# A spectral-routing block with experts on one core: the images of the first stage are normalised by ScalarE, large memsets move behind the folds, and the routing rows take a way through DRAM

## What is computed

```python
# block 1: x = x + conv_ref(layernorm over channels of x)
r = relu(conv1x1(x, rw_fc1)); r = relu(conv1x1(r, rw_conv)); r = conv1x1(r, rw_fc2)
routeing = softmax(r.mean(h, w).reshape(B, 4, 256), axis=1)
s = conv3x3(relu(conv3x3(x, sp_fc1)), sp_fc2)
spatial_routeing = softmax(s.mean(h, w).reshape(B, 4, 256), axis=1)
xp = star_scale * square(relu(x @ w_pw1.T)) + star_bias      # 128 -> 256 channels
xf = rfft2(xp)
weight = einsum('bfc,hwf->bhwc', routeing, complex_weights)
spatial_weight = einsum('bfc,hwf->bhwc', spatial_routeing, spatial_weights)
out = (xp * spatial_weight + irfft2(xf * weight)) @ w_pw2.T  # 256 -> 128 channels
# block 2: t = t + sum over the top 2 of 8 experts of softmax weight * w2(silu(w1 x) * (w3 x))
```

## Time and profile before

| | |
|---|---|
| median of 3 runs | 529.23 us (526.0 to 530.99) |
| span of the profiled execution, first to last instruction | 477.8 us |
| median less that span (what lies around it) | 51.4 us |
| first Fourier matmul of pair 0 | 25.05 us |
| the same of pair 5 | 74.95 us |
| `r_hl` complete | 115.6 us |
| first matmul of the second stage | 130.19 us |

### The profile page before, as it was taken

How to read it: one execution, slowest core, us unless ns; L and a number is a source line. 1 busy time by engine, 2 the same in 40 slices (tenths; PEclk the granted TensorE clock), 3 DMA queues, 4 the chain that set the end, 5 groups by cost and what they waited for, 6 DMA issues and landing times.

```text
span 477.8 us, 8130 instructions
## 1 busy us (share of the span) xinstructions
PE 359.2 (75%) x2236; PEld 292.9 (61%) x2237; DVE 272.9 (57%) x673; ACT 162.8 (34%) x374; POOL 260.3 (54%) x267
## 2 busy tenths in 40 slices
PE   0899999895199988875007699999999999998500
PEld 0555555393058777764006599887987888887400
DVE  5367675614077999996898554444434444433245
ACT  0454543302013223211400355443444444443253
POOL 7333342512176655541650667777777777777444
PEclk9999999978579999999555599999999999998955
DMA  8920000000200000004600111111111111112194
GB/s 249 248 63 1 2 0 0 1 5 9 35 1 1 23 22 32 34 24 152 287 0 1 45 40 54 50 52 49 54 51 49 55 50 49 52 54 50 42 358 162
DMA packets 14081, 29.94 MB, mean 63 GB/s; under 512 B 4392, under 2 KB 5564, under 8 KB 13548
## 3 DMA queue, kind: packets, MB, share of 16 engines
q1 hardware_dynamic: 7388, 17.93, 12.1%
q0 software_dynamic: 4784, 9.52, 6.7%
q10 hardware_dynamic: 1888, 2.23, 1.3%
HBM read 20.24 MB, written 8.85 MB: 61 GB/s over the span
## 4 chain that ended last, share of the span: by engine, by line
PE 35%; DVE 26%; DMA 13%; issue 12%; POOL 8%; ACT 2%; DVEq 1%; POOLq 1%; SPq 1%; ACTq 0%
PE bank L927 8%; DVE xn L964 7%; DMA y_dram<-shared,idx_s 7%; PE bank L909 6%; PE bank L902 3%; DMA RS<-r_hl 3%; PE bank L772 2%; PE bank L715 2%; PE bank L723 2%; POOL shared L490 2%; DVE st L954 2%; DMA shared<-tn_dram,idx_g 2%; PE bank L734 2%; DVE spec L1179 2%; PE bank L888 2%
## 5 line engine op out<-in xcount | busy, mean ns | idle before, releaser
L518 POOL DMA_INDIRECT shared<-tn_dram,idx_g x71 | 68.8, 968 | 39.9 <-DVE idx_g L1217 18.6
L527 POOL DMA_INDIRECT y_dram<-shared,idx_s x71 | 70.0, 986 | 27.1 <-issue 12.8
L909 PE MATMUL bank<-spec,shared 128*128 x426 | 61.2, 280 | 1.8 <-DVE shared L1233 0.7
L1247 DVE TENSOR_TENSOR shared<-shared,bank 128x384 f32<-128x384 f32 x71 | 39.3, 554 | 36.4 <-ACT shared L672 35.4
L672 ACT ACTIVATE shared<-bank 128x384 f32<-128x384 f32 x71 | 34.8, 490 | 64.3 <-PE bank L927 64.3
L909 PEld LDWEIGHTS bank<-spec,shared 128*128 128x128 f32 x426 | 53.5, 193 | 5.1 <-issue 5.0
L927 PE MATMUL bank<-RS,xgt_hl 128*128 x142 | 55.5, 391 | 0.6
L964 DVE TENSOR_SCALAR xn<-T,mv,rstd 128x128 f32<-128x128 f32 (+1 forms) x64 | 51.4, 874 | 5.1 <-POOL rstd L429 4.6
L927 PE MATMUL bank<-w_hi,xgt_hl 128*128 x142 | 48.9, 345 | 0.0
L427 POOL TENSOR_SCALAR var_eps<-mv 128x4 f32<-128x4 f32 x16 | 3.7, 229 | 68.7 <-DVE mv L958 68.6
L1228 DVE TENSOR_TENSOR xgt_hl<-bank,xgt_hl 128x128 fp32r<-128x128 f32 x71 | 20.6, 290 | 33.7 <-ACT xgt_hl L660 33.7
(11 more groups left out here) (171 smaller groups left out, 680.0 us busy)
## 6 DMA issues: line engine op xcount, KB each, us to landing
star<-y_dram SPq DMA_DIRECT2D x16, 256.0 KB, 5.4
star<-in_w SPq DMA_DIRECT2D x2, 1536.0 KB, 8.5
tn_dram<-xn SPq DMA_DIRECT2D x8, 256.0 KB, 2.0
out<-T ACTq DMA_DIRECT2D x8, 256.0 KB, 2.3
spec<-in_w SPq DMA_DIRECT2D x1, 1536.0 KB, 13.2
shared<-in_sp_even SPq DMA_DIRECT2D x1, 1280.0 KB, 13.2
shared<-tn_dram,idx_g POOLq DMA_INDIRECT x71, 2.5
y_dram<-shared,idx_s POOLq DMA_INDIRECT x71, 2.2
```

The lines of the kernel that those rows point to most:

```text
L518: pool.indirect_dma_start(xg[b], None, tn_dram, bass.IndirectOffsetOnAxis(ap=idx_g[quad][:, col:col + 1], axis=0)).then_inc(S[f"g_x{b}"], 16)
L527: pool.indirect_dma_start(y_dram, bass.IndirectOffsetOnAxis(ap=idx_s[quad][:, col:col + 1], axis=0), yo[b], None).then_inc(S[f"y_out{b}"], 16)
L909: mm = pe.matmul(p_y[:, 0:DIM], hidt[u][:, c * P:(c + 1) * P], w2s[:, c, ds(e * DIM, DIM)], start=(c == 0), stop=(c == HC - 1))
L1247: dve.tensor_tensor(hid[u], silu[u], p_h3[u][:, 0:HID], ALU.mult).then_inc(S["f_act"], 1)
```

## The change

Four things are done. (1) ACT writes `xn` in the first stage, as an activation with a scale `rstd` and a bias `shift` = -mean * rstd; POOL computes `neg_mean` and `shift`, two more small operations for each pair. DVE's `normalise` goes from the first stage and stays in the second. (2) ACT does one relu of one column into `table_probe` behind its first four DMAs, so that its table is loaded there. (3) POOL's large memsets, among them that of `RS` (now in two halves), move from ahead of the first fold to behind the folds of pairs 0 and 1. (4) The routing rows go from `r_hl` into a DRAM buffer `r_dram` by two DMAs of 128 KB, and from there into `RS` by four DMAs of 128 KB, each into 8 partitions; all six are issued by SP.

```diff
+        r_dram = nc.dram_tensor("r_dram", (2, 2, NF, PAIRS * 4 * P), F32).ap()
-        def routing_rows(eng, blocks, done):
-            eng.wait_ge(S["r_hi"], 1)
-            eng.wait_ge(S["r_lo"], 1)
-            eng.wait_ge(S["rs_zero"], 1)
-            for r in blocks:
-                eng.dma_start(RS[4 * r:4 * r + 4].rearrange("f c g b m -> f (c g b) m").bitcast(F32),
-                              r_hl[:, r % 2, 1 - r // 4, :].bitcast(F32)).then_inc(S[done], 16)
...
@@ SP @@
-            routing_rows(sp, range(5), "r_rows")
+            sp.wait_ge(S["r_hi"], 1)
+            sp.wait_ge(S["r_lo"], 1)
+            for s in (1, 0):
+                sp.dma_start(r_dram[s].rearrange("h f (x m) -> (f x) h m", m=P), r_hl[:, :, s, :].bitcast(F32))\
+                    .then_inc(S[f"r_out{s}"], 16)
+            sp.wait_ge(S["rs_zero"], 2)
+            for s in (1, 0):
+                sp.wait_ge(S[f"r_out{s}"], 16)
+                for half in range(2):
+                    r0 = 16 * (1 - s) + 8 * half
+                    sp.dma_start(RS[r0:r0 + 8].rearrange("r c g b m -> r (c g b m)").bitcast(F32),
+                                 r_dram[s].rearrange("h f n -> (h f) n")).then_inc(S["r_rows"], 16)
...
@@ POOL @@
                 wait_apart(pool, S[aggr], i + 1)
+                if aggr == "a_aggr":
+                    pool.tensor_scalar(neg_mean[:, u, :], mv[:, u, :, 0], -1.0, None, ALU.mult)
...
+            def neg_shift(i, u):
+                wait_apart(pool, S["a_rstd"], i + 1)
+                pool.tensor_tensor(shift[:, u, :], neg_mean[:, u, :], rstd[:, u, :], ALU.mult).then_inc(S["a_shift"], 1)
+
             def phase_a(i, u):
                 if not last(i, PAIRS):
                     inv_std("a_aggr", "a_eps", "a_rstd", LN_C_EPS, i + 1, 1 - u)
+                    neg_shift(i + 1, 1 - u)
...
-            routing_rows(pool, range(5, 8), "r_rows_pool")
             fold_rows(PAIRS - 1, 1)
...
@@ ACT @@
+            act.wait_ge(S["mhalf_set"], 1)
+            act.activation(table_probe[:, :], mhalf[:, 0:1], ACT.Relu)
             act.wait_ge(S["w_zero"], 3)
             for g in range(2):
                 act.dma_start(rwc[HALF * g:HALF * g + HALF, HALF * g:HALF * g + HALF], io["rwc"])\
                     .then_inc(S["consts_in"], 16)
+            def normalise_image(i, u):
+                act.wait_ge(S["a_shift"], i + 1)
+                for t in range(4):
+                    op = act.activation(xn[:, u, t, :], flat(T[:, ds(i * 4 + t, 1), :]), ACT.Identity,
+                                        scale=rstd[:, u, t:t + 1], bias=shift[:, u, t:t + 1])
+                op.then_inc(S["a_norm"], 1)
...
             def phase_a(i, u):
+                if not last(i, PAIRS):
+                    wait_done(act, S["a_tr"], i)
+                    normalise_image(i + 1, 1 - u)
                 if not deferred(i):
                     star_relu(i)
                     star_square(i)
...
@@ DVE, phase_a @@
-                if not last(i, PAIRS):
-                    wait_done(dve, S["a_tr"], i)
-                    normalise("a", i + 1, 1 - u)
```

More of the change, by code:

```diff
@@ L206, in metaformer @@
         var_eps = sb("var_eps", [P, 2, 4])
+        neg_mean = sb("neg_mean", [P, 2, 4])
+        shift = sb("shift", [P, 2, 4])
+        table_probe = sb("table_probe", [P, 1])
         tri = sb("tri", [P, P], F16)
@@ L326, in metaformer @@
             "ident_in consts_in tab_in x_in0 x_in1 x_in2 x_in3 route_in w1_in w3_in w2_in w_hi w_lo pad_zero coef_zero mhalf_set coef_ps "
-            "coef_hi coef_lo coef_in a_stats a_aggr a_eps a_rstd a_norm a_tr a_xc a_xp a_pw a_conv a_rw1 a_relu_s "
+            "coef_hi coef_lo coef_in a_stats a_aggr a_eps a_rstd a_shift a_norm a_tr a_xc a_xp a_pw a_conv a_rw1 a_relu_s "
             "a_relu_r a_rw2 a_rsum a_rows a_relu a_sq a_star a_fold a_dft a_spec r_cols r_full r_taps r_mm "
-            "r_log r_max r_sub r_exp r_sum r_rec r_norm r_tr r_hi r_lo r_rows r_rows_pool b_w b_sw b_p b_cross b_u b_y "
+            "r_log r_max r_sub r_exp r_sum r_rec r_norm r_tr r_hi r_lo r_out0 r_out1 r_rows b_w b_sw b_p b_cross b_u b_y "
             "b_vt b_vts b_w2 b_t b_stats b_aggr b_eps b_rstd b_norm b_tn0 b_tn1 b_tr b_tnt "
@@ L446, in _ @@
             inv_std("a_aggr", "a_eps", "a_rstd", LN_C_EPS, 0, 0)
+            neg_shift(0, 0)
+            phase_a(0, 0)
             pool.memset(coef[:].rearrange("p c k -> p (c k)").bitcast(F32), 0.0).then_inc(S["coef_zero"], 1)
@@ L454, in _ @@
                                pattern=[[-1, P]], channel_multiplier=1).then_inc(S["q_tri"], 1)
-            pool.memset(RS[:].rearrange("p c g b m -> p (c g b m)").bitcast(F32), 0.0).then_inc(S["rs_zero"], 1)
+            rs_flat = RS[:].rearrange("p c g b m -> p (c g b m)").bitcast(F32)
+            pool.memset(rs_flat[:, 0:2048], 0.0).then_inc(S["rs_zero"], 1)
+            phase_a(1, 1)
+            pool.memset(rs_flat[:, 2048:4096], 0.0).then_inc(S["rs_zero"], 1)
             pool.memset(tap_k[:].rearrange("p t b -> p (t b)"), 0.0).then_inc(S["k_zero"], 1)
             pool.memset(rw_k[:, :], 0.0).then_inc(S["k_zero"], 1)
-            pair_loop(pool, phase_a)
+            with pool.Fori(1, PAIRS // 2 - 1) as n:
+                for u in range(2):
+                    phase_a(n * 2 + u, u)
+            phase_a(PAIRS - 2, 0)
+            phase_a(PAIRS - 1, 1)
             pool.wait_ge(S["a_conv"], PAIRS)
@@ L598, in phase_a @@
                                accum_out=rsum[:, ds(i, 1)]).then_inc(S["a_rsum"], 1)
+            normalise_image(0, 0)
             act.wait_ge(S["pad_zero"], 1)
@@ L784, in _ @@
             pe.wait_ge(S["coef_in"], 16 * 8)
-            pe.wait_ge(S["r_rows"], 16 * 5)
-            pe.wait_ge(S["r_rows_pool"], 16 * 3)
+            pe.wait_ge(S["r_rows"], 16 * 4)
             pe.wait_ge(S["a_relu"], 2 * PAIRS)
@@ L1001, in _ @@
             stats("a", 0, 0)
-            normalise("a", 0, 0)
             pair_loop(dve, phase_a)
```

## The result

The changed kernel takes 545.78 us (median of 4 runs, 539.11 to 546.9) beside 529.45 for the kernel before in the same comparison: ratio 1.0294, 95% interval 1.0226 to 1.0363. It is slower, by 16.3 us; the forecast was 542. Its profiled execution spans 543.1 us.

What follows compares the result with a forecast made beforehand. It took a first-stage ring through statistics, POOL, DVE's `xn` and PE as the bound, with PE nearly so. Start -2.7, ring +15.3, last pass +1.1 and rows -1 gave +12.7: span 490.5 plus 51.4, 542 us; range 533 to 551.

Steps and rivals of the forecast that it cites:

- The ring: First stage: relus waiting for the next pair's `shift` join both paths into one ring, 13.05 us a pass, +15.3 us.
- the first rival: First stage: with relus free of `shift`, the old ring shrinks to 9.1 us a pass, 521 us in all; chance 5%.
- One sign: First-stage loop: PE idle some 4 us a pass, listed among the signs that the prediction is right.
- The clock: First stage: rival that PE's clock falls in some passes, a pass growing by 2 or so, +7 us, 549 us; chance 12%.
- the forecast case: Whole kernel: the prediction's main case, +12.7 us, 542 us; chance 55%.
- The start: Top of the kernel: first `star_matmul` at 12.1 instead of 14.81, held by the landing of the constants, -2.7 us.
- Memsets behind the folds cost nothing: First two folds: memsets of 3.1 and 2.7 us fit into POOL's 3.6 us idle from fold to next means.
- Behind the last pass: Pair 7, statistics to transposes after the last ring pass: 5.0 us instead of 3.93, +1.1.
- The routing rows: From `r_hl` to the filters' matmul: 13.2 us instead of 14.6 by way of DRAM, taken as -1 us.
- The rival of the quick rows: Routing rows: the 512 B pieces were the limit, so the routing saves 8 us instead of 1, 535 us; chance 18%.
- the price by partitions: Reads into `RS`: 8 partitions at a time give 54 GB/s, 2.4 us for 128 KB, 9.7 for four in turn.
- The 51.4 us around the span: Whole run: 51.4 us between the profiled span of 477.8 and the median of 529.23, taken as unchanged.

Runs made afterwards that it cites:

- e_norm_only: Kernel before with only the first stage's normalisation moved to ACT, ahead of the relus, with its two POOL operations: 494.31 us, ratio 1.0342.
- e_norm_behind: Changed kernel with ACT's normalisation of the next pair placed behind the relus and squares instead of ahead: 467.82 us, ratio 0.9803.
- e_warm: Changed kernel with four more matmuls, their results unused, behind the transposes of each pass to keep PE busy: 538.7 us, ratio 1.0192.
- c_after: Changed kernel run again without edit, on a second chip, beside the kernel before: 541.21 us, ratio 1.0223.
- e_start_only: Kernel before with only the early table load and the routing tile's memsets moved behind the first two folds: 529.06 us, ratio 1.0011.
- e_rows_only: Kernel before with only the routing rows sent through DRAM: 473.39 us, ratio 0.9922.
- e_rows32: Kernel with ACT's normalisation behind relus and squares, plus four DRAM writes and one read into all 32 partitions: 515.22 us, ratio 0.9767.

## Why the prediction was right

- **The ring.** Right in its mechanism: `e_norm_only` alone makes the loss, and `e_norm_behind`, with the same work, has a pass of 9.42 us where the first rival had put 9.1. The size was 13.05 a pass, and 13.60 was measured, with the clock's share in it. At full clock the sum by steps was too long by 2.1 us over the five passes: one pass of `e_warm`, from statistics to statistics (49.40 to 62.20), is 12.80 us, and the mean of five 12.62, since the first takes only 12.0. The estimates hold one by one: `neg_mean` and `shift` with `rstd` 2.2 us (2.22 forecast), four activations 1.55 until the relus (1.54), relus and squares 2.1 (2.14). One sign failed: PE was to be idle some 4 us a pass, and was idle 2.5 ((67.98 - 55.29) / 5), because the Fourier matmuls, which count as busy, last longer.
- **The clock.** This is the step that the forecast case had wrong. It put the clock at full throughout; a fall was a rival at 12% with +1.5 a pass, and it happened in four of the five passes, with +1.0 a pass on average. The prediction leaned on the stretch at 220 us, busy 1.18 of 2.00 us at full clock; ahead of the Fourier matmuls stand now, from the end of the transposes (57.38) to 60.97, 3.6 us with only 0.70 of PE's work in them. And the price wasn't on the convolution, as I had costed it, but on the Fourier matmuls, the one piece of PE's work that is on the ring: 2.35 to 3.43. The forecast case has nothing for it: +5 us.
- **The start.** -2.7 forecast, -3.4 measured at pair 2's statistics, partly by a wrong road. The DMAs of `rwc` didn't wait for the table load; they were issued as early as before (2.77), and it was their landing that varied: the star matmul stood at 12.35 in this profile, at 11.15 in `c_after`, the same kernel, and at 10.8 to 11.1 in the others that were ready early. And the gain needs neither the probe nor the moved memsets: `e_norm_only` has it without them, because ACT's own first `xn` loads the table early and isn't held by the memset. `e_start_only` has it too at pair 2 (24.24), by the probe and the memsets, and loses it in the next pass.
- **Memsets behind the folds cost nothing**: right here, but POOL's idle time, on which I rested it, was half of the condition. Where VectorE normalises beside them, the same memsets make a pass 3.9 us longer (`e_start_only`: 13.74 from pair 2 to pair 3, against 9.79, with the fallen clock in it). The Trainium skill, SBUF — State Buffer, "Who interferes with whom", says that VectorE and GpSimd share a pair of ports under an exclusive lock while ScalarE has its own. The traces agree: VectorE's `xn` takes 1.12 us beside an idle POOL, 3.05 beside folds, 5.29 beside folds and memsets, and ends each time just behind POOL's work; ACT's takes 1.65 beside either.
- **Behind the last pass.** Forecast 5.0, measured 5.09.
- **The routing rows.** Forecast -1, measured -3.1 in the gap of the changed kernel, and -1.5 to -2.2 in `e_rows_only`. Read by read, a pitch of 1.9 us, not 2.4: 67 GB/s for 8 partitions, not twice the 27 of four. From the first read's issue to the matmul 9.6 us, where I had 11.1. The rival of the quick rows, 16 KB pieces at full rate, is out; its price was too high as well, since the prediction's own "2.4 plus issues of 0.6 each" comes to about 4.2 in place of 9.7, which saves 6.5 in all and not 8. Each read is 8 packets of 16 KB, which took 1.94 us in the third and fourth read, and the next read's packets start where those of the one before end. Over one whole pitch of the reads (136.90 to 138.85 us of the changed kernel) the DMA share is 0.51:

```profile
136.90:138.85 1.95, 0.00 (x0) 0.00 (x0) 0.00 (x0) 0.00 (x0) 0.00 (x0) 0.50 0.51 67
```

The Trainium skill, DMA: Bandwidth & Descriptors, "Rules for kernel authors", confines a DMA with an outermost dimension of 8 to 8 of 16 engines. The trace agrees: 8 packets at a time, half of the DMA share, and four reads that queue behind one another. So the price by partitions isn't shown by itself: the four reads shared their half of the DMA as well. A packet took 0.9 to 1.6 us in the first of them, 1.9 in the later ones and 0.7 to 1.3 in `e_rows32`; what sets this isn't shown, and a read into 8 partitions that keeps all 16 engines busy, which would tell the two prices apart, wasn't run.

- **The 51.4 us around the span.** Wrong: 1.7 to 1.9 us lie there, in every profiled run but that of before. The rest was, by all that the other profiles show, the experts' stage, longer in the runs than in the profile. Adding it to a span of 490.5 gave the right time only since the runs with which the change was compared had those 50 us too. A span so far from the median of its own kernel's runs should have been a question, not a term.

So the mechanism was right, and the closeness of the number is partly luck. Against the forecast of +12.7 the marks have +5.0 for the clock that I left out, -2.1 for a ring that I had too long, -2.1 at the rows that I had too dear and -0.7 at the start, which comes to nothing, and +12.8 was measured. In the first comparison the difference is 16.3 us, in the two later ones 13.2 and 12.5; the intervals of all three hold 12.8.

## What to carry to other kernels

An instruction moved to an idle engine takes its whole wait with it: ask first what stands behind it in that engine's queue, and put it behind everything that doesn't need its input (one place made 1.03, the other 0.98). When a ring opens gaps on PE, look at the granted clock behind them: here it cost about 1 us a pass, and four matmuls without a use in the gap took that away. And a memset or other POOL work that is "hidden" must, as `e_start_only` shows, be hidden from VectorE as well as from its waiters.

## What the hardware showed that I had not expected

- The granted clock fell at the end of gaps of 3.6 us that held 0.70 us of matmuls (idle pieces of 2.06 and 0.83 us). It stayed up ahead of the one pass whose first idle piece was 0.91 us, where the half clock of the pass before had moved PE's work back into the gap (12.77 after 14.24 us). Four matmuls with no use kept it at 1.00 over all five passes.
- A DMA issue written behind an activation on ACT went out at 2.77 us, during the table load that began at 2.70 for that activation. The activation itself ended at 4.19.
- Reads of 8 packets of 16 KB, issued together, ran one behind another at half of the DMA share (0.51), 1.9 us each.
- The experts' stage took 212 to 214 us in every version on one chip, and 262 to 272 in every version on the others, at 73 and 74 GB/s against 58 to 60. What differs between those chips wasn't tried.
